# One embedding table moves from one-hot matmuls to gathers, and the gathers lose eight waits

## The reference, cut to what matters

```
e = stack([tbl_f[ids[:, f]] for f in range(26)], axis=1)      # 2048 x 26 x 128
c = concatenate([dense[:, None, :], e], axis=1)               # 2048 x 27 x 128
g = einsum('bfd,bgd->bfg', c, c)
z = g[:, iu, ju]                                              # upper triangle, 351
h = relu(concatenate([z, dense], 1) @ W_top1 + b_top1)        # 479 x 512
h = relu(h @ W_top2 + b_top2)                                 # 512 x 256
y = h @ W_top3                                                # 256 x 1
```

## Time and profile before

| | |
|---|---|
| median of 3 runs | 388.1 us (387.46 to 390.06) |
| the profiled execution | 389.89 us, of which the span from first to last instruction is 388.1 us |
| PE busy | 357.7 us, 92% of the span |
| DVE, ACT, POOL busy | 283.2, 158.8, 223.4 us |
| mean granted TensorE clock | 0.978 of full speed |
| turns 2 to 7 | `gram 1` ends at 159, 201.4, 244 ... us, 42.4 us apart |

### The profile page before, as it was taken

One profiled execution on the slowest core, in us unless ns is written; L12 is line 12 of the kernel. 1 busy time (PEld: TensorE's weight loads), 2 busy tenths in 40 slices (PEclk: granted clock), 3 DMA queues, 4 the chain that ended last, 5 costly groups with the idle time before them and its releaser, 6 DMA issues.

```text
span 388.1 us, 14620 instructions
## 1 busy us (share of the span) xinstructions
PE 357.7 (92%) x6468; PEld 338.8 (87%) x6468; DVE 283.2 (73%) x197; ACT 158.8 (41%) x270; POOL 223.4 (58%) x228
## 2 busy tenths in 40 slices
PE   0999877998959999999999999999999999999995
PEld 0888866997949999899889998999989998999894
DVE  3989899990919929697569937895869946993440
ACT  2447542334432344333543344433542445244422
POOL 5755744375723776557664767377654766476500
PEclk9999968999988999999999999999999999999999
DMA  6999313222221222321242212331242113221100
GB/s 183 267 266 282 123 30 105 74 65 51 60 81 49 82 52 63 108 84 49 51 117 65 71 46 74 104 83 49 59 114 83 48 47 121 54 59 49 40 21 2
DMA packets 22607, 33.30 MB, mean 86 GB/s; under 512 B 6111, under 2 KB 14943, under 8 KB 22587
## 3 DMA queue, kind: packets, MB, share of 16 engines
q1 hardware_dynamic: 15234, 18.26, 16.8%
q0 software_dynamic: 7168, 14.69, 14.6%
q10 hardware_dynamic: 186, 0.09, 0.1%
HBM read 29.93 MB, written 0.01 MB: 77 GB/s over the span
## 4 chain that ended last, share of the span: by engine, by line
PE 85%; DMA 5%; issue 4%; SPq 3%; ACT 1%; DVE 1%; DVEq 0%
PE psum L547 45%; PE psum L573 11%; PE psum L562 7%; PE psum L663 6%; DMA lows<-table 5%; PE psum L586 3%; PE psum L588 3%; PE psum L587 3%; PE psum L535 2%; PE psum L671 2%; SPq L236 2%; SPq L203 1%; PE psum L605 1%; DMA pairs<-gram 1%; DVE gram L296 1%
## 5 line engine op out<-in xcount | busy, mean ns | idle before, releaser
L288 POOL DMA_INDIRECT rows<-table,idx x224 | 223.2, 996 | 141.1 <-issue 56.7
L316 DVE TENSOR_TENSOR onehot<-ids_b,psum 125x2048 fp32r<-125x2048 int16 x97 | 216.2, 2280 | 5.8 <-DMA ids_b<-hot_ids 5.3
L406 ACT ACTIVATE feats<-psum 128x512 f32<-128x512 f32 (+2 forms) x120 | 79.6, 711 | 129.7 <-PE psum L547 112.3
L547 PE MATMUL psum<-onehot,hot_hi 125*128 125x256 f32 x736 | 110.9, 295 | 1.4 <-issue 1.2
L547 PE MATMUL psum<-onehot,hot_lo 125*128 125x256 f32 x736 | 103.4, 284 | 0.0
L547 PEld LDWEIGHTS psum<-onehot,hot_hi 125*128 125x128 f32 x736 | 97.3, 195 | 3.0 <-issue 2.0
L296 DVE COPY gram<-psum 26x416 f32<-26x416 f32 x64 | 37.4, 584 | 81.3 <-PE psum L573 79.8
L547 PEld LDWEIGHTS psum<-onehot,hot_lo 125*128 125x128 f32 x736 | 95.7, 193 | 0.0
L573 PEld LDWEIGHTS psum<-feats 128*26 128x26 f32 x4096 | 41.1, 103 | 19.9 <-issue 15.8
L573 PE MATMUL psum<-feats 128*26 128x26 f32 x4096 | 46.5, 193 | 12.9 <-issue 9.4
L406 ACT ACTIVATE gram<-psum 26x416 f32<-26x416 f32 (+1 forms) x72 | 35.6, 494 | 25.2 <-PE psum L573 10.2
(11 more groups left out here) (37 smaller groups left out, 172.4 us busy)
## 6 DMA issues: line engine op xcount, KB each, us to landing
lows<-table SPq DMA_DIRECT2D x12, 448.0 KB
ids_b<-hot_ids SPq DMA_DIRECT2D x8, 512.0 KB
rows<-table,idx POOLq DMA_INDIRECT x224, 2.5
ids_b<-hot_ids SPq DMA_DIRECT2D x8, 256.0 KB
rows<-dense SPq DMA_DIRECT2D x16, 64.0 KB, 3.6
lows<-w SPq DMA_DIRECT2D x1, 1024.0 KB, 24.4
lows<-table SPq DMA_DIRECT2D x12, 52.0 KB
pairs<-gram SPq DMA_DIRECT2D x16, 39.0 KB
```

The costliest lines, as they stand in the source:

```text
L288: pool.indirect_dma_start(out=rows[:, f, :], out_offset=None, in_=tables[f - 1], in_offset=bass.IndirectOffsetOnAxis(ap=idx[:, 2 * s + t, ...
L316: nc.vector.tensor_tensor(onehot[f % SLOTS][0:HP_ROWS, :, :], ids_b[0:HP_ROWS, f:f + 1, :].to_broadcast([HP_ROWS, HC, SB]), psum[0:HP_ROWS ...
L406: return nc.scalar.activation(o, x, ACT.Copy)
L547: mm = nc.tensor.matmul(psum[:, bank, m * SB:(m + 1) * SB], part[0:HP_ROWS, f, c, :], onehot[f % SLOTS][0:HP_ROWS, c, :], start=(part is h ...
```

## The change

`NUM_HOT` goes from 12 to 11: the last hot table (table 23 of the reference) becomes cold. The cold features and the dense row are then 16, four whole groups of four, and a tile has 15 gathers instead of 14. The hot units become four pairs and three single tables, so the ring still has 15 units in a turn and `STEPS` stays. `NOT_BEFORE` and its waits go; the other gates on POOL stay.

```diff
-NUM_HOT = 12
+NUM_HOT = 11
...
-    NOT_BEFORE = {(0, 10): 4, (0, 12): 5, (0, 14): 6, (1, 2): 7, (1, 4): 8, (1, 6): 9, (1, 8): 10, (1, 10): 11}
-
-    HOT = [[f, f + 1] for f in range(0, NH - 2, 2)] + [[NH - 2], [NH - 1]]
+    HOT = [[f, f + 1] for f in range(0, NH - 3, 2)] + [[f] for f in range(NH - 3, NH)]
...
                         for f in features:
-                            if s > 0 and (t, f) in NOT_BEFORE:
-                                pool.wait_ge(hot_done, NH * s + NOT_BEFORE[t, f] + 1)
                             if s > 0 and (t, f) == (0, 6):
```

## The result

The changed kernel takes 377.6 us (median of four runs, 372.8 to 378.8); the kernel before, in four runs beside it, 388.4: faster, by 11 us, a ratio of medians of 0.972. The ratio on record, 0.964 with a 95% interval from 0.954 to 0.974, leaves out the two runs of 378.8, which lie over 1.5% above the fastest one and count as slow; the profiled execution is one of them. The predicted time was 376.0 in a range from 371.5 to 382. The profiled execution took 378.76 us (span 376.9), where the sum had 377.9 for the profiled one.

The account below looks back on a forecast made before the run. PE's instruction list was taken to set the steady time. PE work -13.4, copies +0.35, gathers in `gram 1` +3.3, code stops -2.3 sum to -12.0 us: 377.9 profiled, 376.1 against the median; range 371.5 to 382.

Parts of the forecast that it names:

- PE bounds the kernel, and its list gets shorter: PE's instruction list over eight turns: a table leaves, two transposes come, -1.67 us a turn, -13.4 us in all.
- A gather falls inside `gram 1`: In turns 1 to 6 the last gather starts 0.2 us inside `gram 1`: +0.55 us a turn, +3.3 us.
- Rival A: `gram 1` stays clear of gathers or its hole has another cause; the +3.3 us goes: 372.8 us, chance 0.15.
- `gram 0` unchanged: Two gathers again fall in `gram 0` of a steady turn, so its cost stays at 3.50 us.
- the copies: ACT's longer fourth-group copy before `gram 1`: 0.05 us a turn, between 0 and 0.14, +0.35 us in all.
- No wait in the ring, no wait for rows: PE waits for no bank copy (cover 1.3 us) and no rows 3 of either tile (margins 2.9, 2.7): zero.
- rival C: In the ring of banks PE waits for two copies of 0.83 us a turn, +11.6: 387.7 us, chance 0.05.
- Code stops: PE's issue stops in turns 0 and 1: two vanish (-1.5 and -0.8), those inside grams stay: -2.3 us.
- Rival B: PE's stops for code do not shrink: 378.4 us, chance 0.12; with one more long stop 384.4, chance 0.03.
- moved past four transposes and into layer 1b: The stop at 95.24, near the end of turn 1's `gram 0`, moves ahead of 3 us of slow matmuls: -1.5 us.
- mostly hidden: Skill's claim on crossing instruction block boundaries, rejected by the prediction; at its word, stop terms are 0, sum 2.3 us smaller.
- rival D: POOL's run of 30 gathers becomes the bound; if all are stretched, 47.4 us a turn, 421 us, chance 0.05.

## Why the prediction was right, step by step

*PE bounds the kernel, and its list gets shorter: held.* A single table reads 1.89 us in the chain of the changed kernel, and the steady turns hold PE's work without a hole outside the grams.

*A gather falls inside `gram 1`: held, in place and price; missed by one turn.* It starts 0.15 us inside (forecast 0.2) and costs 0.51 by the run without gathers (0.55 priced). It does so in turns 2 to 6. In turn 1, which the sum had too, the last gather starts at 103.03 and `gram 1` only at 103.72, so the term is 5 times 0.46 = 2.3 us instead of 3.3. Rival A, which took that term away, gave 372.8 and falls with it.

*`gram 0` unchanged: missed, by -0.3 us a turn.* Two gathers start in it, as forecast, but it is 3.2 us and not 3.50. From the single matmuls of both traces, each gather makes two breaks of PE, one of 0.2 us about 0.1 before its row starts, one of 0.27 about 0.4 after. Before, both gathers had both breaks inside the gram; now the first gather starts 0.1 us behind the gram's start (217.55 and 217.46), and its first break falls before the gram. The count of starts was right, and was too coarse a measure. In turn 2 the last gather before the gate starts at 136.11, ahead of `gram 0` at 136.24; that gram shows no break and lost 1.0 us. With the shrunk `gram 0` a steady turn closes: -1.67 + 0.45 for `gram 1` - 0.30 for `gram 0` = -1.52, and -1.44 was measured; the 0.08 left is of the size that the copies were given (0.05), and nothing isolates them.

*No wait in the ring, no wait for rows: held in turns 2 to 6.* The margins of 1.3, 2.9 and 2.7 us were enough on these chips; rival C falls. *In turn 7 missed, +1.0 us*: the long gather of the last tile was in the trace of before, and only the rows of one turn had been laid out. It had cover there, and the shorter PE work uncovered it.

*Code stops: right in sum, wrong in which.* In the two chains they fall from 10.2 to 8.3 us, by 1.8 (2.3 forecast). Where the holes between PE's matmuls at the same places are added up, it is 11.3, 11.3 and 13.0 in the three executions profiled with twelve tables on the first kind of chip (before, its repeat, waits removed), and 9.1, 8.0, 8.9 and 7.5 in the four with eleven tables and all gathers. Rival B, that they would not shrink, falls. The two stops of before that the earlier trace rows does not show, and those of after:

```profile
48.16 2.08 issue
...
62.64 1.75 issue
```

```profile
47.54 1.46 issue
...
61.04 1.19 issue
...
88.22 1.99 issue
...
105.61 3.69 issue
```

The step that failed here is "moved past four transposes and into layer 1b", "Gone: -1.5". The stop of 1.52 did not go; in its place there is one of 1.99 inside `gram 0` of turn 1. Counted over all of PE's instructions (weight loads, matmuls and those of its sequencer), PE's stops stand before at the 705th, 961st, 1473rd, 2497th and 3009th instruction, and after at the 705th, 1473rd, 2241st and 3009th: all of them 193 above a multiple of 256. The Trainium skill's blocks of 256 ("Runtime: NRT & Kernel Launch", "Instruction fetch mechanics") agree with this grid. So does the page of the changed kernel, in its list of DMA queues:

```profile
q8 instruction: 13, 0.21, 0.2%
```

These are 13 packets of 16 KB. Twelve of them start between 34.3 and 110.4 us, among them one at 107.08, within the stop of 3.69; the next starts at 369.7, so the steady turns have none, as they have no stop. A gram is 512 instructions, so two places of the grid lie in it wherever it is shifted. When the last one in `gram 0` was moved out behind its end, the one before it was already inside, at matmul 157 of the gram, and the stop came there. Each of the first four grams, on the first pass through its code, has a stop, in both kernels (1.2 us or longer in this pair, 0.5 and 0.7 us for the second gram of turn 0 in the repeat, where `gram 0` of turn 1 of the kernel before has two). The changed kernel has them at matmuls 152, 244, 157 and 201 of the gram in both executions profiled on the first kind of chip; the run without gathers has one in each of the four grams as well, and a second one in the second. What did go is the short one at 53.20, which stood outside a gram among transposes, for -0.8 us. The rest of the 1.8 us is luck: the three stops that the prediction set at no change became shorter by 1.5 us (2.08 to 1.46, 1.75 to 1.19, 4.00 to 3.69), while 1.52 became 1.99. The Trainium skill's "mostly hidden" does not hold here: 8.3 us of stops are left.

*POOL as the bound, rival D: not on these chips.* In the window above 31 gathers take 28.7 us of 41, at the old distance. On the other kind of chip the kernel does come out slower, but not by D's mechanism: the gathers keep their 1.25 us there (243.13 to 254.37 for ten), and what stretches is the work that waits for others while they run (the copies above, 9.0 us late). The prediction had no such case.

*The sum.* Its -12.0 stands against -11.2 measured in the profiled pair, of which +1.6 is the lower clock at the end of one execution. Without that it is -12.8: better than forecast by `gram 0` (-2.5 over turns 2 to 7) and by the turn without a gather in `gram 1` (-1.0), worse by turn 7 (+1.0), the stops (+0.5) and the load of the first tables, which takes 18.84 us in the chain instead of 18.19 (+0.7). That gives -13.3; the 0.5 left is not assigned, and lies in turns 0 and 1, where the two grams of turn 0 have four gathers instead of one. The right total rests in part on misses that cancel.

## What to carry to other kernels

Lay the events of one engine over the short dense work of another to a tenth of a microsecond: a gather's start 0.1 us earlier or later moved a break out of a gram, and waits whose only effect on a steady turn was where gathers fall cost 1.2 us of 42. When a change has two parts, run each alone: here the part that the prediction's sum rested on, the table, gave 0.3 us a turn beside the other. A shift of code moves stops along a grid and does not remove them where the dense stretch is longer than its pitch. Before trusting a gain from more gathers, time both kernels on several chips: here the sign changed between them.

## What the runs showed of the hardware

- A gather issued by POOL makes PE's stream of small matmuls pause twice, about 0.2 and 0.27 us. Between hot tables' matmuls of 256 columns nothing of it is seen: a turn without gathers is 1.4 us shorter, and the grams account for 1.35 of it.
- PE stops on the first pass through its code at instruction counts that lie 193 above a multiple of 256, for 0.5 to 4.0 us where small matmuls are dense; twelve instruction packets of 16 KB move up to 110 us, and none in the steady turns.
- Two kinds of chips: the same program takes 388 to 389 us on one and 450 to 456 on the other. In the profiled turn on the latter, PE's update reaches the waiting engine 9.0 us after the matmul's end, while ten gathers are under way; on the former it takes 0.01.
- One gather of the last tile takes 3.54 us instead of 0.95, at the same place in every kernel here that gathers it, for a cause not found (turn 0 has others of 2.3 to 3.6 us).
